# Linear attention with a tensor-train FFN on 8 cores: other PSUM banks for the q/k projections, one transpose and one chunk's statistics moved earlier

## The reference

```python
xn = (x - mean(x)) / sqrt(var(x) + 1e-5)            # x: (32, 2048, 1024)
q, k, v = xn @ Wq.T, xn @ Wk.T, xn @ Wv.T           # 16 heads of 64
pq, pk = elu(q) + 1, elu(k) + 1
# scan over the rows t of a sequence, per head:
S = S + outer(pk_t, v_t);  z = z + pk_t
out_t = (pq_t @ S) / (sum(pq_t * z) + 1e-5)
attn = out @ Wo.T + bo
W_real = unfold(G1_R, G2_R); W_imag = unfold(G1_I, G2_I)       # 512 x 512 each
ffn = concat(x_re @ W_real.T - x_im @ W_imag.T + b_re,         # x_re, x_im: halves of xn
             x_re @ W_imag.T + x_im @ W_real.T + b_im)
y = x + attn + ffn
```

## Time and profile before

| | |
|---|---|
| time, median of 3 runs | 2330.24 us (2329.62 to 2331.66) |
| the profiled execution's own time | 2330.57 us |
| its span, slowest core (1) | 2329.0 us; the others 2325.4 to 2328.3 |
| mean granted TensorE clock | 0.850 to 0.851 on all cores |
| busy: PE, DVE, ACT | 1819.8, 968.5, 549.7 us |

### The profile page before, as it was taken

The page is one execution under the profiler, slowest core; times in us unless marked ns, Lnnn a source line. Parts: engine busy times, 40 slices in busy tenths (PEclk is TensorE's granted clock), DMA queues, the critical chain, the costliest instruction groups (busy, mean ns, idle before and its releaser), DMA issues.

```text
span 2329.0 us, 33404 instructions; the slowest of 8 cores (2325.4 to 2329.0 us)
## 1 busy us (share of the span) xinstructions
PE 1819.8 (78%) x11792; PEld 932.1 (40%) x11792; DVE 968.5 (42%) x2148; ACT 549.7 (24%) x885; POOL 11.5 (0%) x23
## 2 busy tenths in 40 slices
PE   2555878787887878787887878788787878788787
PEld 1202434344443434444443444444343444444343
DVE  0155434444434434444443444443443444434343
ACT  2432212122212213221222212221221322122120
POOL 1000000000000000000000000000000000000000
PEclk9999879797988879797887979798887979788797
DMA  7301010101101010111101010110101011110000
GB/s 126 49 1 36 19 55 1 55 19 37 37 19 55 19 37 19 41 33 37 37 19 55 1 55 19 37 37 19 55 19 37 19 39 35 37 37 19 28 1 37
DMA packets 23356, 77.82 MB, mean 33 GB/s; under 512 B 2640, under 2 KB 2656, under 8 KB 23200
## 3 DMA queue, kind: packets, MB, share of 16 engines
q1 hardware_dynamic: 9216, 33.56, 4.7%
q10 hardware_dynamic: 9216, 33.56, 3.9%
q0 software_dynamic: 4768, 8.57, 2.5%
HBM read 50.53 MB, written 33.55 MB: 36 GB/s over the span
## 4 chain that ended last, share of the span: by engine, by line
PE 67%; DVE 20%; ACT 7%; issue 5%; DMA 1%; POOL 0%; DVEq 0%; ACTq 0%; POOLq 0%
PE bP L740 13%; PE bP L681 12%; PE bP L526 10%; PE bP L686 9%; PE bN L526 9%; DVE sc_sb L575 4%; DVE out L710 3%; DVE att_tok L636 3%; ACT pk_tok L772 2%; PE bT L653 2%; ACT v_sb L752 2%; PE bT L490 2%; DVE xn_fm L499 1%; DVE den_t L631 1%; PE bT L339 1%
## 5 line engine op out<-in xcount | busy, mean ns | idle before, releaser
L681 PE MATMUL bP<-wt_Wo,att_fm 128*128 128x512 bf16 x1024 | 283.6, 439 | 67.3 <-ACT v_sb L752 50.7
L740 PE MATMUL bP<-wt_Wv,xn_fm 128*128 128x512 bf16 x1024 | 309.6, 469 | 0.0
L631 DVE TENSOR_SCALAR den_t<-bN 128x4 f32<-128x4 f32 x256 | 41.3, 161 | 489.1 <-PE bN L608 462.0
L686 PE MATMUL bP<-wstg,xn_fm 128*128 128x512 bf16 x1024 | 231.5, 379 | 0.0
L681 PEld LDWEIGHTS bP<-wt_Wo,att_fm 128*128 128x128 bf16 x1024 | 109.4, 111 | 231.7 <-issue 156.6
L575 DVE TENSOR_TENSOR sc_sb<-bS,mask 128x512 bf16<-128x512 f32 x256 | 177.0, 691 | 59.9 <-PE bS L561 52.6
L535 ACT ACTIVATE xn_tok<-bP 128x512 bf16<-128x512 f32 x128 | 76.4, 597 | 483.2 <-PE bP L526 402.3
L740 PEld LDWEIGHTS bP<-wt_Wv,xn_fm 128*128 128x128 bf16 x1024 | 118.4, 118 | 171.3 <-issue 105.9
L752 ACT CAST v_sb<-bP 128x512 bf16<-128x512 f32 x128 | 75.0, 586 | 315.3 <-PE bP L740 313.3
L686 PEld LDWEIGHTS bP<-wstg,xn_fm 128*128 128x128 bf16 x1024 | 100.2, 98 | 120.8
L710 DVE TENSOR_TENSOR out<-bP,x 128x512 f32<-128x512 f32 x128 | 88.5, 692 | 142.2 <-PE bP L694 137.1
(11 more groups left out here) (103 smaller groups left out, 1882.1 us busy)
## 6 DMA issues: line engine op xcount, KB each, us to landing
x<-L_attn_x SPq DMA_DIRECT2D x64, 512.0 KB, 4.6
y<-out ACTq DMA_DIRECT2D x64, 512.0 KB, 4.3
wstg<-L_attn_Wq POOLq DMA_DIRECT2D x1, 2048.0 KB, 18.0
wstg<-L_attn_Wk POOLq DMA_DIRECT2D x1, 2048.0 KB, 29.0
wstg<-L_attn_Wv POOLq DMA_DIRECT2D x1, 2048.0 KB, 17.4
wstg<-L_attn_Wo POOLq DMA_DIRECT2D x1, 2048.0 KB, 17.0
ident<-c_ident POOLq DMA_DIRECT2D x1, 32.0 KB, 6.8
mask<-c_mask POOLq DMA_DIRECT2D x1, 32.0 KB, 7.1
```

What stands on the lines that cost most here:

```text
L681: K.pe(lambda e, ic=ic, bk=bk: e.matmul(bP[bk][:, :], att_fm[:, ic, :], wt["Wo"][:, ic, 512 * bk:512 * (bk + 1)], start=(ic == 0), stop=Fa ...
L686: K.pe(lambda e, kc=kc, bk=bk, cmb2=cmb2: e.matmul(bP[bk][:, :], xn_fm[:, kc, 128 * cmb2:128 * (cmb2 + 1)], m_sb[:, kc, 512 * bk:512 * (bk ...
L740: K.pe(lambda e, kc=kc, bk=bk, cm=cm: e.matmul(bP[bk][:, :], xn_fm[:, kc, 128 * cm:128 * (cm + 1)], wt["Wv"][:, kc, 512 * bk:512 * (bk + 1 ...
```

## The change

Three edits. In `emit_qk` the 16 groups go round bS0, bS1, bP0, bP1 and no longer round bP0, bP1, bN0, bN1. In the start of a macro the transpose of the third chunk is emitted ahead of the third numerator group. The statistics of the next macro's third chunk are emitted at the end of the third chunk and no longer at the end of the fourth.

```diff
--- before.py
+++ after.py
@@ -506,8 +506,8 @@
                 g_xnfm.wrote(*xn_evts)
                 if m == 0:
                     K.wait("pe", wt_evt["Wq"])
-                qk_banks = [bP[0], bP[1], bN[0], bN[1]]
-                qk_guards = [gP[0], gP[1], gN[0], gN[1]]
+                qk_banks = [bS[0], bS[1], bP[0], bP[1]]
+                qk_guards = [gS[0], gS[1], gP[0], gP[1]]
                 esc_slots = [xn_tok[:, 0:512], xn_tok[:, 512:1024],
                              att_tok[0][:, 0:512], att_tok[0][:, 512:1024]]
                 esc_guards = [g_xntok, g_xntok, g_atok[0], g_atok[0]]
@@ -866,9 +866,9 @@
                         emit_out2(c - 2)
                         emit_final2(c - 2)
                         emit_store2(c - 2)
+                        xe[2] = emit_xnT(m, 2, ev_nmr)
                         emit_num_group(b, 2)
                         emit_epi(b, 2)
-                        xe[2] = emit_xnT(m, 2, ev_nmr)
                         emit_num_group(b, 3)
                         emit_epi(b, 3)
                         next_num = c
@@ -943,8 +943,8 @@
                         g_stats[mm % 2].before_write("dve")
                         emit_stats_chunk(mm, 0)
                         emit_stats_chunk(mm, 1)
+                        emit_stats_chunk(mm, 2)
                     elif c % MC == 3:
-                        emit_stats_chunk(mm, 2)
                         emit_stats_chunk(mm, 3)
                         emit_rstd(mm)
                         for cc in range(MC):
```

## The result

The changed kernel takes 2349.5 us (median) against 2330.1 us: ratio 1.0084, 95% interval 1.0073 to 1.0095. In some executions of any of these kernels the cores of one die run at a lower clock and the time is longer; the times from here on are medians without such executions (with them the changed kernel's is 2349.8 us). It is slower, as forecast, but by 19.4 us and not by 53, and the time lies inside the range given and outside the likeliest case's own (2374 to 2392). Of the cases named only "steps in part of the macros only" describes what happened; it shared a chance of 0.06 with another, and had neither a mechanism nor a time.

A forecast was written before the change was run, and what follows sets the result against it. PE, busy 78%, was taken to bound the kernel, with its clock halved in five stretches (44 us) a macro. Terms 51 + 3.3 - 1.8 = +52.5 us on 2330.57 us gave 2383 us; range 2329 to 2393.

The forecast's parts named there:

- the likeliest case: Whole kernel: every macro's period grows by 3.4 us of low clock, 133.12 to 136.5 us; 2383 us, chance 0.58.
- steps in part of the macros only: Whole kernel: the 3.4 us lengthening comes in some macros only; chance 0.06, shared with a 2343 us outcome.
- The new wait: First A_v (L740) after q/k: PE waits for DVE's last L539, 2.37 us, 16 times, 37.9 us.
- one step a macro: Price of the A_v wait: the clock pattern stands 3.4 us later each macro, 15 periods, 51 us.
- the fall in the first A_v: Behind the q/k wait: clock drops for 3.4 us, eight matmuls take twice as long, +1.7 us, delaying A_v's successor.
- the rule for the fall: At the A_v wait: 2.37 us lies nearer to 2.81 (clock fell) than to 1.77 (it did not), so it falls.
- The start gain: Start of q/k: first group in bS0 waits only for the xn_fm copy, 0.73 us less, 15 times, 11.0 us.
- The transpose: xnT(2) ahead of num_group(2): only DVE's order changes; 0 us, bounds 0.69 us either way, 15 times.
- The statistics: At xnT(0): moved statistics shorten PE's wait by 1.70 us, 15 times, 25.5 us before clock effects.
- the cover at the fourth chunk's out2: Where the statistics now stand: the att_fm copy comes later but has 2.1 us of cover before out2; cost 0.
- just this as a rival: At out2: the clock rises one step earlier, 3.4 us less a period, 2280 us without a q/k step; chance 0.08.
- The walk: One macro followed through its clock rises and falls: gains die at rises, the loss stays; period 136.5 us.

The follow-up runs named there:

- the bare wait: Kernel before plus one wait: each macro's first A_v waits for that macro's last L539; banks and orders as before: 2384.8 us, ratio 1.0233.
- the banks with filler: Kernel before with only the new q/k banks, plus nine unread 128x512 matmuls between the last q/k group and the first A_v: 2384.9 us, ratio 1.0235.
- the five matmuls alone: Kernel before plus five unread 128x512 matmuls ahead of xnT(0), nothing else: 2331.1 us, ratio 1.0009.

## Why the prediction was wrong

*The new wait.* Right: its place, its 2.37 us, its 16 times. Its price, put at one step a macro, is right as well: 54.7 us alone against 51 + 3.3 in the sum. That it was right is in part luck. The reason given, the fall in the first A_v, is not needed for it: with the clock held high there the time was the same, and the bare wait cost the same with no such fall. What is shown is that a delay of the second A_v costs one step a macro in each of three ways (the banks, the bare wait, the banks with filler), though the low stretches lie differently in each. Nor was the rule for the fall right, that 2.37 us is nearer to 2.81 than to 1.77: at 2.21 us the changed kernel's clock fell in two kinds of macro and not in the third, and at 2.7 us, in the macro shown, it didn't.

*The start gain.* 0.73 us as read. That it vanishes was wrong where it stands alone: 11 us.

*The transpose.* Nothing, as said.

*The statistics.* The 1.70 us at xnT(0) are right, the cover at the fourth chunk's out2 too. The failing step is "out2 starts at 1375.5 for 1377.21, the rise stays at 1379.8, so 0.85 is left; the next rise (1396.8) halves it to about 0.4". The rise did not stay. With 1.70 us less waiting ahead of it the low stretch ended a step sooner (13.7 us for 17.1), in two macros of three on the changed kernel's slowest core and in nearly all later macros on most cores with the edit alone, and the edit alone gave about 33 us where the step had left about 6. I had listed just this as a rival, with a chance of 0.08, and against it that the numerator group keeps PE waiting. The walk followed one macro at one offset to the clock's pattern, whereas the offset differs from macro to macro as soon as the period is no whole number of steps. The steady periods 126.29, 129.71, 133.12 and 136.53 us are 37, 38, 39 and 40 times 3.413 us, to a hundredth or two. The changed kernel's three (133.18, 135.53, 134.07) are not such multiples, but together they are 402.8 us, 118 times 3.413: it goes round three offsets, and only one of its three macros misses the early rise.

*The sum.* With the measured parts in the place of the estimated ones, 54.7 - 33.5 + 0 = +21.2 against +19.4 measured, no difference that the runs can tell. The forecast's +52.5 is the first term nearly alone.

*What stays open.* What exactly decides whether a shift is halved, kept or turned into a step was not isolated. The bank order bS, bN (one step in three macros for 0.73 us) and the five matmuls alone (none for two early rises) show that the total shift is no guide; the offset at each rise is the likelier guide, and no run isolated it.

The rule of the Trainium skill ("TensorE: Matmul & The Clock Gate", "A second HAM failure mode: psum-queue depth-cycling") points the right way here: waits between groups bought by the choice of PSUM banks cost more than their length, 55 us for 36 us of waiting, while L740's matmuls are still 0.216 us apart where the clock is high (3.45 us for 16 from 1580.82). But the swing that the rule describes did not set the price: with the clock held at 1.00 through the first A_v it was the same (2384.9 us).

## What to carry to other kernels

When PE's clock changes within a loop, measure the loop's period at several rounds first: if it hardly moves with the work, a small edit is worth nothing or a whole stretch in any one macro, and two edits have to be walked through together at more than one offset. When choosing the banks of a stage, let the last ones be those that the next stage does not write. Waits of PE between dense runs can be worth filling with matmuls that nobody reads, if the filled time reaches up to the next dense run (here 64 us, and nothing where a wait of 1.94 us was left between).

## What the runs showed of the hardware

Where TensorE had been at the low clock for 6.8 us around a wait of 2.8 us, it stayed high with nine 128x512 matmuls (1.9 us) in that wait and five more in the earlier one; together they gave 64 us in 15 macros. The nine alone were not run. The five alone gave nothing. One wait of PE, 2.21 us long between the same two dense stages, came with a fall of the clock in two kinds of macro and not in the third. The low stretches within the macros of all these runs lasted 3.4, 6.8, 10.2, 13.7 or 17.1 us, and the steady periods of different kernels were 126.3, 129.7, 133.1 and 136.5 us.
